# The last stage of a layer-plus-experts kernel: the result's stores are issued by ACT instead of SP

## What is computed

```python
x = L0_attn_h                                      # (4, 2048, 256), f32
x = _layernorm(x + _L0_attn_ref(x, ...), axis=-1)
x = _layernorm(x + _L0_ffn_ref(x, ...), axis=-1)   # the second sum is x_acc
return x

def _layernorm(x, axis=-1, eps=1e-05):
    m = jnp.mean(x, axis=axis, keepdims=True)
    v = jnp.var(x, axis=axis, keepdims=True)
    return (x - m) / jnp.sqrt(v + eps)
```

## Time and profile before

| | |
|---|---|
| Median of 3 runs | 1214.69 us (1208.7 to 1215.05) |
| The profiled execution's own time | 1203.26 us |
| Its span in the profile | 1201.4 us |
| Last stage, from the first load's issue to the end of the span | 1156.37 to 1201.4 us |
| PE, DVE, ACT, POOL busy, share of the span | 91%, 76%, 51%, 55% |

### The profile page before, as it was taken

The page is one execution under the profiler, slowest core; times in us unless marked ns, Lnnn a source line. Parts: engine busy times, 40 slices in busy tenths (PEclk is TensorE's granted clock), DMA queues, the critical chain, the costliest instruction groups (busy, mean ns, idle before and its releaser), DMA issues. The chain is left out here.

```text
span 1201.4 us, 22049 instructions
## 1 busy us (share of the span) xinstructions
PE 1087.7 (91%) x6624; PEld 956.4 (80%) x6624; DVE 912.7 (76%) x2050; ACT 617.2 (51%) x1019; POOL 666.7 (55%) x560
## 2 busy tenths in 40 slices
PE   6999999999999998849999999999999999999900
PEld 5778887777777787638888888888888999999900
DVE  5688888888888888736876666777776778888736
ACT  3444444444444443335454555565565666666528
POOL 1111544545454544667666666676684777776434
PEclk9899999999999999859999999999999999999955
DMA  4011222111121121156766656777785889989569
GB/s 158 18 53 53 54 54 54 54 53 53 53 53 53 53 53 36 36 151 169 175 164 153 162 139 154 204 219 183 195 225 150 215 230 258 233 240 238 100 199 379
DMA packets 80243, 164.34 MB, mean 137 GB/s; under 512 B 27568, under 2 KB 44976, under 8 KB 79920
## 3 DMA queue, kind: packets, MB, share of 16 engines
q1 hardware_dynamic: 49968, 127.72, 34.0%
q0 software_dynamic: 30208, 35.81, 16.5%
HBM read 118.78 MB, written 44.70 MB: 136 GB/s over the span
## 5 line engine op out<-in xcount | busy, mean ns | idle before, releaser
L1177 POOL DMA_INDIRECT x_acc<-fy_sb,pair_out x136 | 259.6, 1909 | 116.8 <-issue 51.0
L1367 PE MATMUL fring<-fxh,fw_hi 128*128 128x256 f32 (+1 forms) x704 | 234.5, 333 | 5.0 <-DVE fxl L1281 1.9
L1369 PE MATMUL fring<-fxh,fw_lo 128*128 128x256 f32 (+1 forms) x704 | 233.8, 332 | 0.0
L1368 PE MATMUL fring<-fxl,fw_hi 128*128 128x256 f32 (+1 forms) x704 | 233.1, 331 | 0.0
L1197 ACT ACTIVATE fw_hi<-w_raw 128x1024 fp32r<-128x1024 f32 x156 | 163.6, 1054 | 97.3 <-PE fy L1412 88.6
L1259 DVE TENSOR_TENSOR fw_lo<-w_raw,fw_hi 128x1024 fp32r<-128x1024 f32 x156 | 189.4, 1218 | 14.7 <-ACT fw_hi L1197 14.2
L545 POOL TENSOR_TENSOR rs<-ve,neg_half 128x4 f32<-128x4 f32 x48 | 55.6, 1159 | 256.4 <-DVE nm L632 256.4
L98 POOL DMA_INDIRECT xg<-x_src,pair_in x136 | 155.4, 1143 | 75.0 <-issue 42.2
L88 POOL DMA_INDIRECT slot_list<-pairs,slot_u x128 | 145.9, 1140 | 50.5 <-issue 34.8
L869 PE MATMUL ring<-xh,w_hi 128*128 128x512 f32 x384 | 160.8, 419 | 2.2 <-issue 2.0
L1410 PE MATMUL fy<-fw_hi,gh 128*128 128x256 f32 x544 | 155.7, 286 | 0.0
(11 more groups left out here) (149 smaller groups left out, 2012.1 us busy)
## 6 DMA issues: line engine op xcount, KB each, us to landing
w_raw<-w_ffn SPq DMA_DIRECT2D x156, 512.0 KB, 4.8
x_in<-h SPq DMA_DIRECT2D x16, 512.0 KB, 3.3
x_src<-x SPq DMA_DIRECT2D x16, 512.0 KB, 4.6
x_acc<-x SPq DMA_DIRECT2D x16, 512.0 KB, 5.8
acc<-x_acc SPq DMA_DIRECT2D x16, 512.0 KB, 7.1
out<-o SPq DMA_DIRECT2D x16, 512.0 KB, 6.0
xg<-x_src,pair_in POOLq DMA_INDIRECT x136
x_acc<-fy_sb,pair_out POOLq DMA_INDIRECT x136, 4.7
```

The costliest lines, as they stand in the source:

```text
L1177: nc.gpsimd.indirect_dma_start(x_acc, bass.IndirectOffsetOnAxis(pair_out[j][:, q, 0:1].bitcast(U32), 0), y[j][:, q, :], None, compute_op=A ...
L1367: nc.tensor.matmul(out, hi, rows_hi, start=dc == 0, stop=False)
L1368: nc.tensor.matmul(out, hi, rows_lo, start=False, stop=False)
L1369: last = nc.tensor.matmul(out, lo, rows_hi, start=False, stop=dc == DC - 1)
```

## The change

```diff
@@ first_block, attention_phase
                 for par in range(2):
+                    sp.wait_ge(s_st[par], 32 * (EARLY // 2))
                     sp.wait_ge(s_sc[par], SCAT * (EARLY // 2))
                 sp.dma_start(kept.pair_in[0][:, :, :], slot_list[bass.ds(slot_row, CH), :]
@@ norm_phase, SP
-            def store(n):
-                row = n * ROWS
-                sp.wait_ge(s_o, n + 1)
-                sp.dma_start(out_rows[row:row + ROWS, :].rearrange("(p q) d -> p q d", p=P),
-                             o[n % DEPTH][:, :, :]).then_inc(s_out[n % DEPTH], 16)
-
-            for n in range(DEPTH):
+            for n in range(STEPS):
                 load(n)
-            for n in range(STEPS):
-                store(n)
-                if n + DEPTH < STEPS:
-                    load(n + DEPTH)
-            for j in range(DEPTH):
-                sp.wait_ge(s_out[j], 16 * (STEPS // DEPTH))
@@ norm_phase, ACT
                 last.then_inc(s_o, 1)
+                row = n * ROWS
+                act.wait_ge(s_o, n + 1)
+                act.dma_start(out_rows[row:row + ROWS, :].rearrange("(p q) d -> p q d", p=P),
+                              o[j][:, :, :]).then_inc(s_out[j], 16)
+            for j in range(DEPTH):
+                act.wait_ge(s_out[j], 16 * (STEPS // DEPTH))
```

## The result

Over 22 runs each, in turn on the same chips, the kernel before takes 1215.12 us in the median and the changed one 1220.85. The ratio is 1.0044, with a 95% interval of 1.0025 to 1.0063. The change makes the kernel slower by about half a per cent, some 6 us. One of the 22 runs with the change (1227.26 us) was in a slower state; the medians count it, the ratio leaves it out.

What follows compares the result with a forecast made beforehand. The last stage was taken to be bound by DVE and ACT, within 3% of each other. Steps of 2.61 and 2.52 us made 40.65 against 34.17, and 1214.69 + 6.5 = 1221.2 us, range 1212.8 to 1227.3.

Steps and rivals of the forecast that it cites:

- The bound: Last stage: DVE takes 2.13 us a step, ACT's four instructions 2.07, so ACT has 0.06 us to spare.
- What is taken away: SP loses 16 issues of 0.34 us; loads start 0.39 us earlier, but nobody waits for them: worth nothing.
- The sum: Last stage, ACT's first instruction to last store: 40.65 us against 34.17, 6.5 us added; chance 0.60.
- wait for its own last: ACT, behind each step's four instructions: waiting for its own last one costs 0.06 us.
- issue, first eight steps: ACT's store issue while SP issues a load at the same semaphore value: 0.43 us each.
- issue, other steps: ACT's store issue in the remaining steps: 0.34 us each, as on SP's queue.
- to the next instruction: ACT, from the end of a store's issue to the next instruction's start: 0.05 us, as in SP's queue.
- The wait in `first_block`: New wait for the last stores in `first_block`: costs nothing, since those stores were issued some 40 us earlier.
- The collision of the two issues: Rival, first eight steps: ACT's issue queues behind SP's, 0.82 instead of 0.43 us, 9.6 us in all; chance 0.20.
- The nearly free issue: Rival, last stage: the DMA occupies ACT only 0.03 us, steps of 2.21 us, 1.1 us gained in stage time; chance 0.15.
- The faster case: Rival, last stage: loads no longer behind stores keep the path fuller, at most 0.38 us off, 1214.3; chance 0.05.
- the DMA share in the middle: Sign that the forecast is right: in the middle of the last stage the DMA share falls below 1.0.

Runs made afterwards that it cites:

- The kernel with three tiles: Changed kernel, ACT making three of each step's four tiles, the fourth left out; 33.78 us from ACT's first instruction to the last store's start.
- the bare wait: Kernel before, stores on SP, ACT waiting for its own last instruction behind each step; 34.25 us from ACT's first instruction to last store's start.
- the finer waits: Kernel before, DVE waiting for one tile's statistics at a time instead of all four; ratio to before 0.9991, 32.97 us to the last store's start.
- a step late: Changed kernel, ACT issuing store n - 1 behind step n's four instructions; 34.21 us to the last store's start, ratios to before 1.0009 and 0.9997.

## Why the prediction was right, point by point

**The bound.** It rested on ACT having 0.06 us to spare in a step. The kernel with three tiles and the one with the bare wait show it from both sides: with half a microsecond more slack the stores are free, and the bare wait, which makes a step 2.07 us and a few hundredths, still fits. The 0.06 us is what is left once every step is finished before the next begins, which is the case that the change makes. An ACT that keeps running has more: four starts 0.495 us apart make 1.98 us, and with the finer waits it did run at 1.97, so it has 0.15 us to spare.

**What is taken away is worth nothing.** Right. Loads were issued sooner, SP's issues became shorter, and DVE waited for one load only, as before.

**The sum.** Forecast 40.65 us for the stretch, measured 40.11: added 5.9 where 6.5 was forecast. The terms, by the chain above:

| Term, us | forecast | measured |
|---|---|---|
| four instructions | 2.07 | 2.07 to 2.08 |
| wait for its own last | 0.06 | 0.03 (0.02 in the chain, which counts 2.08 for the four) |
| issue, first eight steps | 0.43 | 0.39 once, then 0.36 |
| issue, other steps | 0.34 | 0.34 |
| to the next instruction | 0.05 | 0.05, and 0.10 to 0.11 ahead of the ninth step and all later ones |

The wait was taken too dear: ACT's own count reaches its queue as fast as it reached SP, not as slowly as on POOL. The issue at the same moment as SP's load was 0.36 and not 0.43, so 0.02 longer than in the other steps, not 0.09. What I had left out is an instruction of its own: from the ninth step ACT must also wait for an older store. Before, that wait lay beside running instructions; behind a drained step it costs 0.06 us. Eight times 0.06 too little and, in the other terms, about 1.0 us too much left the forecast 0.5 us high.

**The other costs.** The wait in `first_block` is free, as said, and shown by itself.

**The rivals.** The collision of the two issues did not come: 0.39 us was the most on ACT, and SP's loads of the same moments took 0.33. Of the lock that was feared at most 0.02 us shows. The nearly free issue is wrong for this order of the instructions, but not for the reason I weighed. The issue is not short; it is free when something is running. I had not seen that ACT's queue runs ahead of ACT, and so not that the loss belongs to the place of the issue and not to the engine. The faster case did not come either: loads started sooner, and DVE had not been waiting for them. An engine of its own for the outputs gained nothing in either place: 5.9 us lost behind the step, and the old 34.2 us for the stretch a step late.

**What would show it.** ACT's sixteen pieces, their distance, the issue's length and DVE's end came out. One sign hardly came out: I said the DMA share in the middle would fall below 1.0. It does so from 1182.5 to 1186.5 (0.88), but is 1.01 from 1186.5 to 1190.5 and 1.02 to 1.03 in the next 12 us. The prediction took 1.05 MB in 2.6 us, 403 GB/s; at the measured 2.51 us a load and a store ask for 418, no less than the 409 that the path moves there. It falls to 0.80 only behind the last load, which is issued at 1198.1. The time did not depend on it.

**The numbers.** The forecast was 1221.2 us in a range of 1212.8 to 1227.3, and 1220.85 was measured. That the two agree to 0.4 us is luck: the sum was 0.5 us high, it was added to a median of three runs, and twelve more runs of the changed kernel gave 1222.45. What the prediction earned is the 5.9 against 6.5 us in the stretch. The case lies so near half a per cent that the two measurements, 1.0044 and 1.0066, fall on either side of it.

## What to carry to other kernels

- Before moving a DMA's issue to the engine that makes its data, subtract that engine's time per step from the pace of the stage. Here 0.06 us of slack meant a loss of 0.4 us in every step, and half a microsecond meant next to none; the queue that was relieved had nobody waiting for it.
- If the issue must be on a busy engine, put it one step late in that engine's list. Its wait then no longer finds the engine empty, the transfer still starts at the same moment, and sixteen issues of 0.35 us cost nothing.
- Where runs scatter by 15 us and the change is worth 6, read the one stretch that the change touches: the seven executions (of six kernels) in which four instructions a step keep DVE's pace gave 34.17 to 34.25 us, wherever in the execution their last stage began.
